# Maxima of two units in one reduction over two PSUM banks, in the last of three attention blocks

## The chip, the cores and the metric

One core of a Trainium2 chip runs the whole program. The metric is device time in microseconds, from one launch to its end. Three runs of the kernel before are shown, and one more execution was taken with a profile.

## The reference

A decoder-like stack of four layers over tokens `x` of shape (4, 256, 256). Each layer adds a gated cross-attention over a context of shape (4, 512, 256), and then a gated feed-forward, each behind a layer norm. The attentions of layers 0, 2 and 3 have 16 heads of 16 columns; that of layer 1 is a plain memory read. The feed-forwards of layers 0, 1 and 3 are mixtures of experts, that of layer 2 has weights of signs. What the change touches most is the attention of layer 3:

```python
def rms_norm(x, g, eps=EPS): ...
ctx_img, ctx_txt = context[:, :IMG_LEN], context[:, IMG_LEN:]      # IMG_LEN = 257 of 512
q = rms_norm(x @ Wq + bq, gq).reshape(b, -1, n, d)
k = rms_norm(ctx_txt @ Wk + bk, gk).reshape(b, -1, n, d)
k_img = rms_norm(ctx_img @ Wk_img + bk_img, gk_img).reshape(b, -1, n, d)
img_x = _attend(q, k_img, v_img)              # softmax over 257 keys
txt_x = _attend(q, k, v, k_mask)              # another softmax over 255 keys
out = (txt_x + img_x).reshape(b, -1, n * d)
return out @ Wo + bo
```

There are two softmaxes per query and head, one over the first 257 keys and one over the other 255, and so two maxima.

## The kernel before

The whole stack is one program. Tokens stay in SBUF; every block is written as a list of steps, and each engine runs through the same list and does its own part of each step, in that order. Nothing else orders the work but semaphores. Blocks are numbered 0 to 3, batches (of 256 tokens) `c` or `b` 0 to 3.

**Attention.** A batch has `UNITS_OF_BATCH` = 32 units of each of two kinds:

- Maxima, step `("mx", b, k)`: TensorE multiplies one tile of 128 queries of one head with all 512 keys into one PSUM bank (L886), and VectorE reduces the bank to its negated maximum. In block 3 (`two`) that is two reductions, over columns 0 to 256 (L1368) and 257 to 511 (L1369); in block 2 it is one over 512 (L1371). Block 0 has no maxima.
- Scores, step `("sc", c, u)`: the product turned round (keys on partitions, L877), of which ScalarE takes the exponential (L1059, L1061). Four units further on, `("wg", c, part)` multiplies the exponentials with the values (L910); in block 3 a `wg` has 16 or 24 small matmuls in turn. `ev` copies the sums out.

The maxima run `LAG` = 26 units ahead of the scores, since they take a detour: `ng` (VectorE splits them in two halves of precision), `nt` (TensorE turns them), `ne` (ScalarE copies), `nw` (SyncE writes them to DRAM), `nr` (GpSimd reads them back into rows beside the queries, so that the score matmul subtracts them). This is done once for each half of a batch.

Around these the list has the preparation of the next batches: `ln`, `lm` (layer norm; its root is taken by GpSimd), `xt`, `xe` (turned tokens), `kp`, `sq`, `ms`, `kk`, `tk`, `te` (keys in natural order, squares, root by GpSimd, normalization at L1289, turned), `q`, `tq`, `qe` (queries), `v`, `ve` (values), `kw`, `qw` (SyncE writes keys and queries to DRAM), `kr`, `qr` (GpSimd loads them back, the last index is the half). `("qr", 0, 1)` is followed on GpSimd's queue by a memset of the other query buffer (L628) and loads of constant rows. Behind the scores come `dt`, `dd` (sums turned, divided), `ot`, `oe`, `wo`, `wd` (projection out).

**Positions.** `order(blk)` gives each step a number and sorts: `mx` k of batch c stands at 32c + k, `sc` u at 32c + u + 26.5, `wg` at 4 part + 33.6. Preparation stands at 32c plus the offset in `PREP`, for batch 1 with `FIRST_SHIFT` added; the steps after the scores at an offset in `FINISH`. `FOLLOW` places the statistics, the transposes and the routing of the next feed-forward. Steps in `LEADS` are run early, between the tiles of the feed-forward before; `HOOKS` puts the first and last steps of an attention between tiles of a feed-forward, and `MISC` holds the small offsets.

**Banks.** A step that fills PSUM takes the next bank of its ring. `RING_A[3]` = (2, 3) serves `mx`, `dt` and `wo`, `RING_B[3]` = (5, 6, 7) the other fills. `emptied(blk, fill)` names the event that gives a bank back, and the next fill of that bank waits for it on TensorE (`wait_bank`). For a maxima unit this is its own last reduction, counted in `mx_done`.

Of the kernel before, what the change touches and what calls it, by code (L numbers as in the profile page):

```python
# [37 lines left out]
M = 512  # L38
# [53 lines left out]
def hooks(first, *lists):  # L92
# [12 lines left out]
HOOKS = [{0: [("late", "ot"), ("late", "oe")], 1: [("late", "wo")], 2: [("late", "wd"), ("late", "wr")],  # L105
         3: [("late", "wn")], 4: [("statistics", 1)], 5: [("normal", 1)],
         6: [("turn", 1), ("halves", 1)], 7: [("logits", 1)], 8: [("route", 1, 0)],
         9: [("route", 1, 1)], 10: [("route", 1, 2)], 11: [("weights", 1)], 12: [("combine", 1)],
         15: [("add", 0)], 16: [("mem", "scale"), ("extra", 0), ("extra", 1)],
         17: [("mem", "round")], 18: [("mem", "diag")], 19: [("mem", "whole")],  # L110
         20: [("mem", "spread")], 21: [("mem", "normal")], 22: [("mem", "turn")],
         23: [("mem", "context0")], 24: [("mem", "context1")], 25: [("mem", "mask")],
         26: [("mem", "kept")]},
         {-1: [("logits", 0), ("route", 0, 0), ("route", 0, 1), ("route", 0, 2)],
         0: [("weights", 0), ("combine", 0)], 1: [("statistics", 1)],
         2: [("normal", 1), ("turn", 1)], 3: [("halves", 1), ("logits", 1)], 4: [("route", 1, 0)],
         5: [("route", 1, 1)], 6: [("route", 1, 2)], 7: [("weights", 1)], 8: [("combine", 1)],
         11: [("add", 0)]},
         {0: [("late", "ot"), ("late", "oe")], 1: [("late", "wo")], 2: [("late", "wd")],
# [3 lines left out]
         3: [("statistics", 1)], 4: [("normal", 1)], 5: [("turn", 1)], 6: [("halves", 1)],  # L123
         7: [("logits", 1)], 8: [("route", 1, 0)], 9: [("route", 1, 1)], 10: [("route", 1, 2)],
         11: [("weights", 1)], 12: [("combine", 1)], 26: [("add", 0)]}]
# [180 lines left out]
def emptied(blk, fill):  # L306
# [29 lines left out]
    if name == "wo":  # L336
        return "wo_done", ("wd", b)
# [2506 lines left out]
```

How the kernel before makes its waits and increments, by code:

```python
    def wait(eng, kind, n):  # L596
        if isinstance(n, int) and n <= 0:
            return
        eng.wait_ge(sems[kind], n)
# [1 line left out]
    def link(eng, name, ins):  # L602
        chain[name] += 1
        ins.then_inc(sems[name], 1)
        eng.wait_ge(sems[name], chain[name])
# [20 lines left out]
    def zero_stack(eng, stack):  # L627
        then(eng.memset(stack[:, :].bitcast(F32), 0.0), "q_zeroed")
        zeroed[0] += 1
        eng.wait_ge(sems["q_zeroed"], zeroed[0])
# [23 lines left out]
        def w(eng, kind, n):  # L654
            if kind[:2] == "f_":
                ff_wait(eng, blk, kind, n)
            elif n > 0:
                eng.wait_ge(sems[kind], n + before_attention("pw" if kind[:2] == "pw" else kind, blk))
# [71 lines left out]
        def wait_loaded(eng, b, ph):  # L731
            eng.wait_ge(sems[f"d_r{buf(b)}{ph}"], landed(blk, b))
            if b < 2:
                wait(eng, f"d_au{buf(b)}", constants(blk, buf(b)))
                eng.wait_ge(sems["q_zeroed"], {0: 2, 2: 3 + b, 3: 4 + min(b, 1)}[blk])
                eng.wait_ge(sems["s_zeroed"], 1)
# [12 lines left out]
            def wait_weights(mat):  # L750
                if blk == 0:
                    eng.wait_ge(sems["w0_l"], {WK: 1, WQ: 2, WV: 3, WO: 4}[mat])
                    if mat in (WV, WO):
                        eng.wait_ge(sems["bias_l"], 2)
                elif blk == 2:
                    eng.wait_ge(sems["w2_l"], 2)
                    eng.wait_ge(sems["bias_l"], 2)
                    if mat == WQ:
                        eng.wait_ge(sems["q_tc"], 2)
```

## Time and profile before

| | us |
|---|---|
| median of three runs | 1186.84 |
| lowest and highest | 1183.28, 1188.63 |
| the profiled execution | 1182.87 |
| its span, first to last instruction | 1181.0 |

The mean granted TensorE clock of the profiled execution was 0.945 of full speed. Durations and starts below come from this one execution; starts count from the beginning of the span. The last attention block takes its maxima from about 742 to 912, and the feed-forward before it ends near 730.

### The profile page before, as it was taken

The numbers are of one execution on the slowest core, as the hardware profiler recorded it, in microseconds if no ns is written. First come the engines' busy times: TensorE is split into PE (matmuls) and PEld (weight loads), VectorE is DVE, ScalarE is ACT, GpSimd is POOL, SyncE is SP. The second block draws the span as 40 slices with busy tenths as digits, with TensorE's granted clock in tenths as the row PEclk, the third lists the DMA queues.
The fourth block names the chain that finished last, engine by engine and source line by source line (L and its number), as shares of the span: only waits on it lengthen the run. The fifth ranks groups of instructions, "written<-read, shape, count | busy, mean of one in ns | idle before, by whom it ended". The sixth has DMA issues, their size and how long they took to land.

```text
span 1181.0 us, 19127 instructions
## 1 busy us (share of the span) xinstructions
PE 1021.6 (87%) x6456; PEld 767.5 (65%) x6456; DVE 800.9 (68%) x1639; ACT 570.5 (48%) x1129; POOL 380.6 (32%) x423
## 2 busy tenths in 40 slices
PE   4799878999888897779999876699999989999998
PEld 3566546877766686655665565365655578887887
DVE  6477759567866367578887675677766365676676
ACT  2677753444433343316567543146555545444443
POOL 5312214355303245331211231422110043554553
PEclk8999989999988899879999998699999999999999
DMA  6957523554320277685640254927240144555544
GB/s 201 260 134 171 124 71 103 168 156 126 116 90 4 80 140 189 168 155 136 140 98 21 68 107 134 193 54 172 86 92 4 30 132 123 157 153 159 147 151 129
DMA packets 87050, 145.85 MB, mean 124 GB/s; under 512 B 10413, under 2 KB 42438, under 8 KB 84538
## 3 DMA queue, kind: packets, MB, share of 16 engines
q1 hardware_dynamic: 77562, 111.36, 31.6%
q0 software_dynamic: 9408, 33.45, 15.9%
q8 instruction: 47, 0.77, 0.3%
q14 instruction: 33, 0.27, 0.1%
HBM read 113.41 MB, written 32.41 MB: 123 GB/s over the span
## 4 chain that ended last, share of the span: by engine, by line
PE 54%; DVE 16%; DMA 9%; issue 7%; ACT 6%; POOL 5%; SPq 2%; DVEq 0%; ACTq 0%; POOLq 0%
PE psum L617 33%; PE psum L910 6%; PE psum L877 5%; PE psum L886 5%; DMA ff_raw<-in_ff 5%; ACT probs L1059 2%; DMA weights_out<-combine 2%; DVE nmx L1371 1%; POOL ff_wl L1955 1%; DVE nmx L1368 1%; DVE nmx L1369 1%; DVE ff_s L1994 1%; PE psum L836 1%; POOL keys L1122 1%; DMA keys<-keys_out 1%
## 5 line engine op out<-in xcount | busy, mean ns | idle before, releaser
L617 PE MATMUL psum<-ff_xh,ff_wh 128*128 128x512 f32 x424 | 177.7, 419 | 33.9 <-POOL ff_wl L1955 29.9
L2011 DVE TENSOR_TENSOR ff_hl<-ff_h,ff_hh 128x512 fp32r<-128x512 f32 x114 | 121.8, 1069 | 98.4 <-ACT ff_hh L1896 97.8
L1061 ACT ACTIVATE probs<-psum 128x512 f32<-128x512 f32 x256 | 144.6, 597 | 86.1 <-PE psum L877 82.3
L1955 POOL TENSOR_TENSOR ff_wl<-ff_raw,ff_wh 128x512 fp32r<-128x512 f32 x92 | 120.5, 1310 | 173.2 <-ACT ff_wh L1907 173.1
L877 PE MATMUL psum<-queries,keys 128*128 128x512 f32 x384 | 153.4, 429 | 12.2 <-ACT probs L1059 7.4
L617 PE MATMUL psum<-ff_xh,ff_wl 128*128 128x512 f32 x392 | 157.1, 401 | 0.0
L1907 ACT ACTIVATE ff_wh<-ff_raw 128x512 fp32r<-128x512 f32 x92 | 58.0, 630 | 183.1 <-DMA ff_raw<-in_ff 181.0
L617 PE MATMUL psum<-ff_wh,ff_hh 128*128 128x256 f32 x456 | 131.5, 292 | 10.3 <-DVE ff_hl L2011 10.3
L886 PE MATMUL psum<-keys,queries 128*128 128x512 f32 x256 | 119.6, 484 | 15.6 <-DVE nmx L1369 8.9
L617 PE MATMUL psum<-ff_wh,ff_hl 128*128 128x256 f32 x456 | 130.5, 290 | 0.0
L617 PEld LDWEIGHTS psum<-ff_xh,ff_wh 128*128 128x128 f32 x424 | 83.3, 196 | 58.0 <-POOL ff_wl L1955 35.9
L1960 POOL TENSOR_TENSOR ff_wl<-ff_raw,ff_wh 128x256 fp32r<-128x256 f32 x92 | 90.3, 982 | 75.1 <-ACT ff_wh L1914 73.9
L1994 DVE TENSOR_TENSOR ff_s<-ff_s,ff_w 128x512 f32<-128x512 f32 x98 | 96.7, 986 | 25.2 <-ACT ff_s L1920 18.7
L910 PE MATMUL psum<-probs,values 128*32 128x256 f32 x1664 | 111.6, 390 | 2.1 <-DVE probs L1462 1.9
L617 PE MATMUL psum<-ff_wl,ff_hh 128*128 128x256 f32 x392 | 113.4, 289 | 0.0
L617 PEld LDWEIGHTS psum<-ff_wh,ff_hh 128*128 128x128 f32 x456 | 91.1, 200 | 19.1 <-issue 12.9
L877 PEld LDWEIGHTS psum<-queries,keys 128*128 128x128 f32 x384 | 69.4, 189 | 51.2 <-ACT probs L1059 22.6
L886 PEld LDWEIGHTS psum<-keys,queries 128*128 128x128 f32 x256 | 51.2, 203 | 64.5 <-DVE nmx L1369 31.0
L1059 ACT ACTIVATE probs<-psum,aug 128x512 f32<-128x512 f32 x128 | 80.9, 692 | 24.2 <-PE psum L877 23.9
L617 PEld LDWEIGHTS psum<-ff_wh,ff_hl 128*128 128x128 f32 x456 | 90.6, 199 | 0.5
L1896 ACT ACTIVATE ff_hh<-ff_h 128x512 fp32r<-128x512 f32 x114 | 70.9, 622 | 35.5 <-DVE ff_h L2000 31.6
L1371 DVE TENSOR_REDUCE nmx<-psum 128x1 f32<-128x512 f32 x128 | 80.6, 682 | 10.7 <-PE psum L886 10.5
(263 smaller groups left out, 2154.8 us busy)
## 6 DMA issues: line engine op xcount, KB each, us to landing
ff_w<-weights_out SPq DMA_DIRECT2D x94, 256.0 KB
ff_raw<-in_ff SPq DMA_DIRECT2D x92, 256.0 KB, 3.6
keys_out<-keys_turned SPq DMA_DIRECT2D x36, 512.0 KB, 4.4
keys<-keys_out POOLq DMA_DIRECT2D x48, 384.0 KB, 7.5
ff_raw<-in_ff SPq DMA_DIRECT2D x106, 128.0 KB, 2.1
queries_out<-queries_turned SPq DMA_DIRECT2D x36, 256.0 KB, 3.2
queries<-queries_out POOLq DMA_DIRECT2D x32, 256.0 KB, 4.3
w_raw<-in_w SPq DMA_DIRECT2D x12, 256.0 KB, 3.7
```

The lines of the kernel that those rows point to most:

```text
L617: last = eng.matmul(dst, lhs[i](k), rhs[j](k), start=start and n == 0, stop=stop and n == groups * len(pairs) - 1, skip_group_check=True)
L877: then(eng.matmul(dst, kst[buf(c)][:, pair, kt * P:(kt + 1) * P], qst[buf(c)][:, :, pair, :], start=True, stop=True, skip_group_check=True ...
L886: then(eng.matmul(bank(st), qst[buf(b)][:, m, pair, qt * P:(qt + 1) * P], kst[buf(b)][:, pair, :], start=True, stop=True), "mx_full")
L910: last = eng.matmul(psum[32 * j:32 * j + 32, SUM_BANK, col:col + S], values[:, c % 2, slot, h * VW:h * VW + 32], probs[:, n % 3, i, j, :], ...
L1059: ins = eng.activation(dst, src, ACT.Exp, scale=SCALE, bias=aug0[:, KT * c + kt:KT * c + kt + 1])
L1061: ins = eng.activation(dst, src, ACT.Exp, scale=SCALE)
L1371: ins = eng.tensor_reduce(at_(0), bank(st), AX.X, ALU.max, negate=True)
L1896: then(eng.activation(ff_hh[:, slot, :], ff_h[:, slot, :], ACT.Copy), "f_hh")
L1955: then(eng.tensor_tensor(ff_wl[:, slot, 0:2 * D], raw(n, slot)[:, 0:2 * D], ff_wh[:, slot, 0:2 * D].bitcast(F32), ALU.subtract), "f_w1r")
L1960: then(eng.tensor_tensor(ff_wl[:, slot, 2 * D:3 * D], raw(n, slot)[:, BD:BD + D], ff_wh[:, slot, BD:BD + D].bitcast(F32), ALU.subtract), " ...
L1994: then(eng.tensor_tensor(ff_s[:, slot, :], ff_s[:, slot, :], ff_w[:, slot, :], ALU.mult), "f_sw")
L2011: then(eng.tensor_tensor(ff_hl[:, slot, :], ff_h[:, slot, :], ff_hh[:, slot, :].bitcast(F32), ALU.subtract), "f_hr")
```

## The change

In block 3 the two units of a pair (k even and k odd) get neighbouring places, at the odd one's position, and lie in banks 2 and 3. VectorE does nothing at the even unit. At the odd one it takes the maximum over columns 0 to 256 of both banks in one reduction with an output of 128 x 2, and then the same for columns 257 to 511. Both banks count as emptied when both reductions of the pair are over. Where the ring is shifted by an odd number of `wo` fills, the even unit lies in bank 3; TensorE then takes the tile of queries that belongs to the bank (`qt = plan.bank[st] - min(RING_A[blk])`). The number of maxima matmuls is the same; 256 reductions become 128.

Besides, positions change in every block: hooks in all four feed-forwards, offsets of preparation, of loads from DRAM and of values in blocks 0, 2 and 3, the shift of batch 1 in block 3 from -6.6 to +3.2, and the place of the routing. In the order that results for block 3, the loads of batch 0 (`kr`, `qr`) and the maxima 0 and 1 stand ahead of `xt`, `kp` and the rest of batch 1; the even and odd maxima are followed by two scores each time; `ct` stands behind the last `wg`. No step is added or dropped.

```diff
-         {0: [("late", "ot"), ("late", "oe")], 1: [("late", "wo")], 2: [("late", "wd")],
+         {0: [("late", "ot")], 1: [("late", "oe")], 2: [("late", "wo"), ("late", "wd")],
...
-         3: [("statistics", 1)], 4: [("normal", 1)], 5: [("turn", 1)], 6: [("halves", 1)],
-         7: [("logits", 1)], 8: [("route", 1, 0)], 9: [("route", 1, 1)], 10: [("route", 1, 2)],
-         11: [("weights", 1)], 12: [("combine", 1)], 26: [("add", 0)]}]
+         3: [("statistics", 1), ("normal", 1)], 4: [("turn", 1)], 5: [("halves", 1)],
+         6: [("logits", 1)], 7: [("route", 1, 0)], 8: [("route", 1, 1)], 9: [("route", 1, 2)],
+         10: [("weights", 1)], 12: [("combine", 1)], 26: [("add", 0)]}]
...
-        ("qr", 0, -8.8), ("kr", 1, -0.5), ("qr", 1, -8.3), ("v", 0, 5.2), ("ve", 0, 5.8), ("v", 1, 8.2),
+        ("qr", 0, -4.8), ("kr", 1, 5.9), ("qr", 1, -1.9), ("v", 0, 7.6), ("ve", 0, 8.2), ("v", 1, 10.6),
...
-        ("kr", 0, -12), ("qr", 0, -13.4), ("kr", 1, -0.5), ("qr", 1, -1.5), ("v", 0, 19.5), ("ve", 0, 20.1),
-        ("v", 1, 22.5), ("ve", 1, 32.3)],
+        ("kk", 2, -22), ("tq", None, -19.2), ("qe", None, -18.6), ("qw", None, -17.2), ("kr", 0, -14.4),
+        ("qr", 0, -13.4), ("kr", 1, 7.5), ("qr", 1, -1.5), ("v", 0, 19.5), ("ve", 0, 20.1), ("v", 1, 23.7),
+        ("ve", 1, 25.7)],
 }
-FIRST_SHIFT = {0: -16.4, 2: -14, 3: -6.6}
+FIRST_SHIFT = {0: -16.4, 2: -14, 3: 3.2}
...
-FOLLOW = {0: (17.6, 4.6, 18.8), 2: (26.2, 9.2, 0), 3: (25.6, 9.2, 23.2)}
+FOLLOW = {0: (17.6, 4.6, 20), 2: (30.2, 9.2, 0), 3: (25.6, 9.2, 25.6)}
...
-                at(r + k, "mx", c, k)
+
+                at(r + (k // 2 * 2 + 1 - (1 - k % 2) * .005 if blk == 3 else k), "mx", c, k)
...
         return "wo_done", ("wd", b)
+    if blk == 3:
+
+        return "mx_done", ("mx", b, rest[0] | 1)
     return "mx_done", fill
...
             def maxima(st):
                 _, b, k = st
                 pair, m, qt = k // 4, k // 2 % 2, k % 2
+                if two:
+
+                    qt = plan.bank[st] - min(RING_A[blk])
...
-                if b and k % HALF_UNITS == 0:
+                if two and qt == 0:
+                    return
+                if b and k // 2 * 2 % HALF_UNITS == 0:
                     w(eng, "neg_done", HALVES * (b - 1) + ph + 1)
                 filled(eng, st)
 
-                def at_(part):
-                    i = (part * JJ + jj) * QT + qt
-                    return nmx[:, ph, m, i:i + 1]
-
                 if two:
-                    eng.tensor_reduce(at_(0), bank(st)[:, 0:IMG], AX.X, ALU.max, negate=True)
-                    ins = eng.tensor_reduce(at_(1), bank(st)[:, IMG:M], AX.X, ALU.max, negate=True)
+                    banks = psum[:, min(RING_A[blk]):min(RING_A[blk]) + QT, :]
+                    i = jj * QT
+                    then(eng.tensor_reduce(nmx[:, ph, m, i:i + QT], banks[:, :, 0:IMG], AX.X, ALU.max, negate=True),
+                         "mx_done")
+                    i += JJ * QT
+                    ins = eng.tensor_reduce(nmx[:, ph, m, i:i + QT], banks[:, :, IMG:M], AX.X, ALU.max, negate=True)
                 else:
-                    ins = eng.tensor_reduce(at_(0), bank(st), AX.X, ALU.max, negate=True)
+                    i = jj * QT + qt
+                    ins = eng.tensor_reduce(nmx[:, ph, m, i:i + 1], bank(st), AX.X, ALU.max, negate=True)
                 then(ins, "mx_done")
```

## Rows read from the trace of the kernel before

**Rows 1.** The page: busy time of each engine, its share, its instructions.

```profile
PE 1021.6 (87%) x6456; PEld 767.5 (65%) x6456; DVE 800.9 (68%) x1639; ACT 570.5 (48%) x1129; POOL 380.6 (32%) x423
```

**Rows 2.** Windows: us, busy (x) PE PEld DVE ACT POOL, PEclk, DMA share, GB/s.

```profile
742.00:760.00 18.00, 10.51 (x35) 6.22 (x33) 11.23 (x32) 1.96 (x7) 6.75 (x10) 0.62 0.98 208
781.00:912.00 131.00, 122.79 (x977) 78.29 (x977) 94.17 (x277) 75.79 (x159) 21.52 (x40) 1.00 0.33 80
```

**Rows 3.** Waits in 781:912: us in total, times, longest.

```profile
PEld psum L886 <- DVE nmx L1369: 17.6, 36, 1.3
```

**Rows 4.** Timeline, 813 to 821: two groups of four units (start, length, engine).

```profile
813.59 0.50 PE L886 MATMUL psum<-keys,queries 128*128 128x512 f32 x1
...
817.26 0.50 PE L886 MATMUL psum<-keys,queries 128*128 128x512 f32 x1
...
817.60 0.40 PE L877 MATMUL psum<-queries,keys 128*128 128x512 f32 x1
...
817.80 0.42 DVE L1368 TENSOR_REDUCE nmx<-psum 128x1 f32<-128x257 f32 x1 [0.90 <-PE psum L886]
817.84 0.39 PE L886 MATMUL psum<-keys,queries 128*128 128x512 f32 x1
...
818.14 0.41 DVE L1369 TENSOR_REDUCE nmx<-psum 128x1 f32<-128x255 f32 x1
...
818.61 0.50 PE L886 MATMUL psum<-keys,queries 128*128 128x512 f32 x1
...
819.94 1.50 PE L910 MATMUL psum<-probs,values 128*32 128x256 f32 x24
...
821.37 0.50 PE L886 MATMUL psum<-keys,queries 128*128 128x512 f32 x1
```

**Rows 5.** Lines by form on VectorE: block 2's reduction and the last block's first.

```profile
L1371 DVE TENSOR_REDUCE nmx<-psum 128x1 f32<-128x512 f32 x128 | 80.6, 682 | 10.7 <-PE psum L886 10.5
...
L1368 DVE TENSOR_REDUCE nmx<-psum 128x1 f32<-128x257 f32 x128 | 54.7, 436 | 37.6 <-PE psum L886 37.2
```

**Rows 6.** Timeline, 872 to 880: the units around the turned outputs.

```profile
872.91 0.50 PE L886 MATMUL psum<-keys,queries 128*128 128x512 f32 x1
...
879.63 0.50 PE L886 MATMUL psum<-keys,queries 128*128 128x512 f32 x1
```

**Rows 7.** Timeline of SyncE's queue, 716 to 750.

```profile
721.89 1.41 SPq L1516 DMA_DIRECT2D queries_out<-queries_turned  x3
```

**Rows 8.** Transfers from issue to landing, 710 to 745 (KB each, median us).

```profile
queries<-queries_out POOLq DMA_DIRECT2D x4, 256.0 KB, 3.9
...
keys<-keys_out POOLq DMA_DIRECT2D x2, 384.0 KB, 7.0
```

**Rows 9.** Timeline of the opening of the last attention block, 731 to 749.

```profile
731.41 0.69 POOL L1113 TENSOR_TENSOR rstd<-ve,half_neg 128x2 f32<-128x2 f32 x1 [12.99 <-DVE ve L1254]
732.06 1.15 POOL L1122 DMA_DIRECT2D queries<-queries_out  x2
732.14 0.73 DVE L1262 TENSOR_SCALAR xn<-x,mv,rstd 128x256 f32<-128x256 f32 x2 [0.81 <-POOL rstd L1113]
...
740.33 3.56 POOL L628 MEMSET queries<- 128x4096 f32 x1
...
741.61 0.73 PE L886 MATMUL psum<-keys,queries 128*128 128x512 f32 x2 [0.99 <-DMA keys<-keys_out]
...
742.15 1.77 DVE L1368 TENSOR_REDUCE nmx<-psum 128x1 f32<-128x257 f32 x1
...
748.49 0.88 DVE L1289 SCALAR_TENSOR_TENSOR kn<-psum,rms,rows 128x256 f32<-128x256 f32 x2 [4.57 <-POOL rms L1116]
```

**Rows 10.** Timeline of TensorE, 753 to 762: two maxima matmuls, low clock.

```profile
757.43 1.45 PE L886 MATMUL psum<-keys,queries 128*128 128x512 f32 x2 [1.13 <-DVE nmx L1369]
```

**Rows 11.** Timeline of ScalarE: the block's first exponentials.

```profile
776.84 1.28 ACT L1061 ACTIVATE probs<-psum 128x512 f32<-128x512 f32 x2 [6.12 <-PE psum L877]
```

**Rows 12.** Timeline of TensorE before the last feed-forward.

```profile
942.72 0.60 PE L1721 MATMUL psum<-ident_r,rt_c 128*17 128x128 f32 x4 [0.48 <-DVE rt_c L1706]
```

More of the change, by code:

```diff
@@ L101 @@
         3: ("ot", "oe", "wo", "wd")}
[L105 to L113, printed above, removed]
+HOOKS = [{0: [("late", "ot"), ("late", "oe")], 1: [("late", "wo")], 3: [("late", "wd"), ("late", "wr")],
+         4: [("late", "wn")], 5: [("statistics", 1), ("normal", 1)],
+         6: [("turn", 1), ("halves", 1)], 8: [("logits", 1), ("route", 1, 0), ("route", 1, 1)],
+         10: [("route", 1, 2)], 11: [("weights", 1)], 12: [("combine", 1)], 15: [("add", 0)],
+         16: [("mem", "scale"), ("extra", 0), ("extra", 1)], 17: [("mem", "round")],
+         18: [("mem", "diag"), ("mem", "whole")], 19: [("mem", "spread")], 20: [("mem", "normal")],
+         21: [("mem", "turn")], 22: [("mem", "context0")], 23: [("mem", "context1")],
+         24: [("mem", "mask")], 25: [("mem", "kept")]},
          {-1: [("logits", 0), ("route", 0, 0), ("route", 0, 1), ("route", 0, 2)],
-         0: [("weights", 0), ("combine", 0)], 1: [("statistics", 1)],
-         2: [("normal", 1), ("turn", 1)], 3: [("halves", 1), ("logits", 1)], 4: [("route", 1, 0)],
-         5: [("route", 1, 1)], 6: [("route", 1, 2)], 7: [("weights", 1)], 8: [("combine", 1)],
+         0: [("weights", 0), ("combine", 0), ("statistics", 1)], 1: [("normal", 1)],
+         2: [("turn", 1), ("halves", 1)], 3: [("logits", 1)], 4: [("route", 1, 0)],
+         5: [("route", 1, 1)], 6: [("route", 1, 2)], 7: [("weights", 1)], 9: [("combine", 1)],
          11: [("add", 0)]},
-         {0: [("late", "ot"), ("late", "oe")], 1: [("late", "wo")], 2: [("late", "wd")],
+         {0: [("late", "ot")], 1: [("late", "oe")], 2: [("late", "wo"), ("late", "wd")],
          3: [("late", "wn")], 4: [("statistics", 1)], 5: [("normal", 1), ("extra", 0)],
@@ L225, in check_order @@
     assert asked == taken, blk
-MISC = {"au": -20, "ng": 0.3, "nt": 1.8, "ne": 2.3, "nw": 2.4, "nr": 2.5, "cl": 1.4, "ev": 0.3, "fx": 3.5, "fw": 3, "fv": 32, "fe": 1.2, "lg": 4, "ro1": 1.5, "ro2": 3.5, "ct": 6, "ce": 6.8}
+MISC = {"au": -20, "ng": 0.9, "nt": 2.1, "ne": 2.3, "nw": 2.4, "nr": 2.5, "cl": 1.4, "ev": 0.3, "fx": 3.5, "fw": 3, "fv": 32, "fe": 1.2, "lg": 4, "ro1": 1.5, "ro2": 3.5, "ct": 6, "ce": 6.8}
 def order(blk):
```

17 rows, old and new, of tables (FINISH, LEADS, PREP) are left out of this document.

## The prediction

> **What bounds the kernel now.** I read the page first: TensorE is busy 87% of the span and VectorE 68% [rows 1]. That is an average over seven blocks, and the main edit touches only the stretch in which the last attention block takes its maxima, so I read that stretch by windows [rows 2]. The reader should see two different regimes. From 742 to 760 TensorE is busy 10.5 of 18 us at a granted clock of 0.62, the DMA engines are busy 98% of the time, and VectorE is not full either: a latency regime. From 781 to 912 TensorE is busy 94% of the time at a clock of 1.00 and VectorE 72%: TensorE's queue is nearly full there, and what it loses it loses in short waits. The view of waits names the main one: 36 times, 17.6 us in all, a weight load for a maxima matmul waited for VectorE's second reduction [rows 3]. The timeline then shows how that wait works [rows 4].
>
> **A group of four units before.** A maxima matmul starts at 817.26, VectorE starts to read at 817.80, its two reads start 0.34 apart, the second ends at 818.55, and at 818.61 TensorE refills the same bank [rows 4]. While VectorE reads one bank TensorE fills the other, so with VectorE limiting a unit costs 2 x 0.34 = 0.67 us. The group from 813.59 to 817.26, with the shorter weighing, takes 3.67 us, the one from 817.26 to 821.37, with the longer, 4.11 us. In the weighing (819.94 to 821.37, 1.43 us) VectorE runs dry and TensorE works.
>
> **Part 1, the reads themselves.** 128 units x 2 reads become 64 x 2, of twice the width. A read of 257 has a mean of 436 ns and one of 512 of 682 ns [rows 5], about 0.96 ns a column, so from the 0.34 us spacing of two 257-column reads a 514-column read should keep VectorE 0.34 + 257 x 0.00096 = 0.59 us, call it 0.60. A pair of units then costs 1.20 us of VectorE for 1.34, which is 0.14 x 64 = 9 us of VectorE time over the block, but VectorE is the limit in only part of it. Bounds: 0.68 a read (two banks cost the same as two reads; saving nothing) and 0.55.
>
> The Trainium skill, page "VectorE: DVE Perf Modes", section on the TRN2 errata, gives a read from PSUM as 120 cycles plus one per element at 0.96 GHz: an estimate from it is 0.39 us for 257 and 0.66 us for 514, so 0.25 us saved per pair and 16 us over 64 pairs. The recorded lengths agree with it (0.41 to 0.42 for 257), but the spacing of 0.34 shows that reads overlap, and so the saving by that page is too high.
>
> **Part 2, the ring of two banks.** The price of the wide read: it needs both banks full, and neither may be refilled until both reads are over (a unit's release is now the odd unit's). From the first matmul of a pair: the second starts 0.34 later [rows 4], is done about 0.40 after that (a matmul that follows another: 0.40, same rows), VectorE starts 0.04 after that, reads for 0.60 + 0.68, and TensorE goes on 0.06 later: 0.78 + 1.28 + 0.06 = 2.12 us from pair to pair, whatever TensorE has in between. Two units cost 1.34 before. In between the new order gives TensorE two score matmuls and, in every other pair, a weighing. With four matmuls at 0.23 to 0.34 (817.26, 817.60, 817.84 [rows 4]) and a weighing of 1.43 a pair takes about 2.5 (TensorE's own), with two scores alone 2.12 (1.2 of it idle). The shorter weighing (1.0) makes it 2.12 too. So a group goes from 4.11 to 2.5 + 2.12 = 4.6, and from 3.67 to 4.24: about +0.5 each. I went through the new order of 781 to 912, 24 groups: some 12 have nothing but scores and weighings (+6 us). Some 8 have a projection, keys or values in the bare pair, which hides the wait entirely and also the 0.3 to 0.4 us waited there now (-3). In two batches turned outputs share the ring with the maxima. There a pair, a turned output, its division on VectorE and the next pair go one after the other: 872.91 to 879.63 holds four units in 6.7 us [rows 6], and by the same steps I get 10.1 (two stretches, one half covered by a projection: +5.5). Sum +8.5 us; bounds +3 (fillers cover more) and +16 (all 24 groups +0.5, both output stretches in full, reads at 0.68).
>
> **Part 3, the opening.** The new order (values of PREP and FIRST_SHIFT) has the key and query loads of batch 0 ahead of the statistics on GpSimd's queue, and the maxima of batch 0 ahead of the preparation of batch 1 on TensorE's. Now: the queries are out by 721.89 + 1.41 plus landing [rows 7], GpSimd has been idle for 13 us, and still the load goes out at 732.06, since GpSimd waits for the root of the layer norm; keys land 7.0 us after issue, queries 3.9 [rows 8]; the first maxima matmul waits for that until 741.61 and VectorE first reads at 742.15 [rows 9]. After: the keys can go at about 720 and the queries at about 727, so both are in by 731; TensorE has no other work then, and VectorE is free after its normalization, at 732.14 + 0.73 = 732.9. That is 9.3 us earlier. The memset of 3.56 us and its loads, which stand now between a request and its root and leave VectorE idle for 4.57 us before 748.49, move ahead to about 733, where no root is asked for: -4.6. Against that: 13 pairs before the first score instead of 26 single units. About 7 have preparation behind them, 6 do not. At the low clock two maxima matmuls take 1.45 us [rows 10] and a pair takes 1.45 + 1.28 + 0.06 = 2.8 instead of the 1.65 of now: 6 x 1.15 = +6.9, or 6 x 0.78 = +4.7 at the full clock; I take +6. The preparation that VectorE did before 742 (two subtractions of 512 columns, by the nearest row 0.68 each [rows 5], a normalization like the 0.88 at 748.49, a small request) now stands in its queue between maxima: +2.4. The narrower reads: 13 x 0.14 = -1.8. Sum -9.3 - 4.6 + 6 + 2.4 - 1.8 = -7.3, I take -7.5. The first exponential, now at 776.84 [rows 11], needs the first half of the maxima back from DRAM; even with no idle time on VectorE it could not come before some 765, so the gain is at most 12; below, 3 if the clock stays low throughout.
>
> **Part 4, the rest.** The turn of the routing weights goes behind the last weighing: the 0.60 us and the 0.48 us of wait in front of it [rows 12] leave the path to the first loads of the last feed-forward, -1 us (0 to -1.1). The loads of the second halves of the keys are asked for about 8 to 10 units later than now; eight units are some 9 to 10 us against a landing of 7.0: hidden, and 1 to 3 us per batch if not. The moves of hooks in the four feed-forwards and of a few reads in blocks 0 and 2 shift an equal set of instructions by one tile or a few units; nothing is added or removed, and the nearby work covers them: 0, bounds -3 and +3.
>
> **The sum**: -7.5 + 8.5 - 1 + 0 = 0 on the profiled execution of 1182.87 us (span 1181.0). The median of the runs shown is 1186.84, 4.0 above it, and it is on this that I put the forecast: 1186 us.
>
> **The rivals.** Faster: the ring costs little (+2, the fillers cover nearly all bare pairs and VectorE's relief helps the work queued behind it) and the opening gives its upper end (-11): 1186.8 + 2 - 11 - 1 = 1177. For it speaks that preparation and weighings are spread through the order and that VectorE stands at 72%; against it the count of bare pairs. Slower, by the clock: TensorE now idles 1 us in every second pair, and if the clock, 1.00 from 781 to 912, falls to its lower level there, two maxima matmuls that take 0.34 + 0.40 = 0.74 at the full clock take 1.45 [rows 10]. From 742 to 760 the clock was 0.62 with TensorE busy 58%. Twenty us of it at half speed cost 10: 1196. It decides from about 12 us on. Against it: the busy share would fall only to some 85%. The Trainium skill, page "TensorE: Matmul & The Clock Gate", section "A second HAM failure mode: psum-queue depth-cycling", says that cycling through PSUM banks with small idles between groups of matmuls makes the clock swing; this is that pattern. Slower, by the loads: the second halves of the keys come 2 us late in three batches, +6, so 1193. That the wide read saves nothing (0.68) is inside the range of part 2.
>
> **How the numbers follow.** Forecast 0.44 (1181 to 1192), faster rival 0.31, clock 0.15, late loads 0.10. What a measurement of this kernel can tell from no change is about 0.5%, 6 us. Faster 0.31, same 0.44, slower 0.25. The range goes from 1174, a little beyond the faster case, to 1199, beyond the clock.
>
> **What would show it.** Part 1: wide reads spaced 0.59 to 0.61 apart. Part 2: pairs of maxima matmuls 2.1 us apart with only scores between, 781 to 912 lengthened from 131 to about 139. Part 3: the first maxima reduction near 733, the first exponential of the block near 768 instead of 777, no 4.57 us wait for the root. The prediction is wrong if the clock falls below 1.00 in the middle of the block, if the wide reads take under 0.5 or over 0.7, or if the opening keeps waiting for the keys.

## The result and the profile after

The change made the kernel faster: 1172.36 us median (1169.49 to 1180.05, 4 runs) against 1185.07 us (1183.28 to 1188.63, 4 runs) for the kernel before beside it, a ratio of 0.990 [0.985, 0.995]. A second measurement of the same kernel, below, gave 0.992 [0.989, 0.995]. The forecast was 1186 us, no difference to be measured; its range began at 1174, and the time lies just under it. The profiled execution after took 1180.05 us (span 1178.2), the longest of its four, so lengths of stages are compared here and the totals are left to the medians.

The lines of after answer to those of before so: maxima matmul L886 to L892, first and second reduction L1368 and L1369 to L1374 and L1377, scores L877 to L880, weighing L910 to L916, and L617, the matmul of the feed-forwards and projections, to L620. The page of after (busy time, share, instructions), for [rows 1]:

```profile
PE 1017.6 (86%) x6456; PEld 768.6 (65%) x6456; DVE 796.2 (68%) x1511; ACT 571.3 (48%) x1129; POOL 383.1 (33%) x423
```

VectorE has 128 instructions fewer, and TensorE has as many as before. The averages say nothing of where the time went, so I cut both executions at the same events. The end of a feed-forward is here the start of VectorE's last product in it (`ff_h`), and the last feed-forward is counted from its first such product to its last. Stage lengths in us, worked out from these events in the two timelines:

```
stage                                                     before   after   after - before
start to the memset ahead of feed-forward 1                368.5   365.4    -3.1
feed-forward 1, from that memset to its end                131.6   118.4   -13.2
block 2: end of feed-forward 1 to last maxima              138.6   137.8    -0.8
block 2: last maxima to end of feed-forward 2               83.7    83.6    -0.1
last block, opening: to the first maxima reduction          19.8    14.7    -5.1
last block, lead: to the first exponential                  34.7    32.6    -2.1
last block, middle: to the last maxima reduction           135.8   153.5   +17.7
last block, tail: to the last feed-forward                  44.1    43.8    -0.3
last feed-forward                                          216.2   220.2    +4.0
```

The last block as a whole is 10 us longer. The gain is in feed-forward 1, which the prediction had at nothing. The first and last stages vary between executions of kernels that are the same there (the first took 365.4, 367.1 and 372.7 us in experiments 5, 6 and 3 below, the last 215.6 in the second profile of the changed kernel), so they carry no argument. The eight us behind the last stage hold the last matmuls, the addition and the store.

**The opening and the lead.** Timeline of after, 713 to 722, against [rows 9]:

```profile
713.10 1.07 POOL L1128 DMA_DIRECT2D queries<-queries_out  x2 [8.88 <-DMA queries_out<-queries_turned]
...
714.32 0.71 POOL L1119 TENSOR_TENSOR rstd<-ve,half_neg 128x2 f32<-128x2 f32 x1 [0.16 <-DVE ve L1260]
...
716.06 3.55 POOL L631 MEMSET queries<- 128x4096 f32 x1
...
720.00 0.68 DVE L1374 TENSOR_REDUCE nmx<-psum 128x2 f32<-128x514 f32 x1
```

The load now stands ahead of the root and waits for nothing but its data (8.88 us idle, ended by the store of the queries). The memset starts 10.8 us behind the end of the feed-forward (705.3) where it stood 18.0 behind it (722.4) before. The first read comes at 720.00, and the first exponential at 752.62, so the two stages are 7.2 us shorter. The store of the queries takes longer to land than it did. Transfers (KB each, median us from issue to landing), 716 to 750 of before and then 699 to 725 of after:

```profile
queries_out<-queries_turned SPq DMA_DIRECT2D x3, 256.0 KB, 2.5
```

```profile
queries_out<-queries_turned SPq DMA_DIRECT2D x3, 256.0 KB, 6.3
```

In after the load of the keys, asked for at 703.11, is under way at the same time. No run separates the two transfers, so that this is the reason is not shown.

**The middle.** Windows of after (columns as in [rows 2]):

```profile
752.00:780.00 28.00, 23.86 (x187) 16.36 (x185) 19.74 (x39) 16.69 (x41) 6.07 (x12) 1.00 0.28 63
780.00:810.00 30.00, 23.50 (x170) 14.86 (x163) 14.19 (x29) 13.75 (x27) 4.96 (x9) 0.89 0.61 139
810.00:840.00 30.00, 26.67 (x214) 17.78 (x213) 21.55 (x47) 16.53 (x40) 4.72 (x9) 1.00 0.39 109
840.00:870.00 30.00, 24.90 (x197) 16.08 (x199) 16.82 (x32) 14.30 (x27) 6.25 (x12) 0.99 0.48 92
870.00:906.00 36.00, 32.37 (x243) 19.57 (x235) 22.81 (x47) 19.61 (x37) 2.05 (x3) 0.96 0.01 3
```

TensorE is busy 131.3 of 154 us where before had 127.3 of 136 (window 777 to 913): its idle time went from 9 to 23 us. The granted clock, 1.00 before, falls to 0.89 between 780 and 810 and to 0.96 behind 870. Timeline of one pair with little behind it (two scores and a short transpose, L851), and below the one matmul that waited for a load:

```profile
835.23 0.62 PE L892 MATMUL psum<-keys,queries 128*128 128x512 f32 x2
...
835.89 0.69 DVE L1374 TENSOR_REDUCE nmx<-psum 128x2 f32<-128x514 f32 x1 [0.67 <-PE psum L892]
...
836.50 0.68 DVE L1377 TENSOR_REDUCE nmx<-psum 128x2 f32<-128x510 f32 x1
...
837.32 0.70 PE L892 MATMUL psum<-keys,queries 128*128 128x512 f32 x2 [0.22 <-DVE nmx L1377]
```

```profile
785.72 1.22 PE L892 MATMUL psum<-keys,queries 128*128 128x512 f32 x2 [3.67 <-DMA keys<-keys_out]
```

From pair to pair it is 2.09 us; 852.71 and 854.73 in the same trace are 2.02 apart. VectorE, which paced the units before, now waits for TensorE (0.67 us here) as TensorE waits for VectorE. The reads by form (busy, mean ns, idle before), for [rows 5]:

```profile
L1374 DVE TENSOR_REDUCE nmx<-psum 128x2 f32<-128x514 f32 x64 | 44.3, 692 | 52.4 <-PE psum L892 51.5
L1377 DVE TENSOR_REDUCE nmx<-psum 128x2 f32<-128x510 f32 x64 | 43.4, 678 | 0.0
```

In all 64 pairs the second read starts 0.60 to 0.61 us after the first.

The fall of the clock behind 870 has no load ahead of it. It stands where turned outputs and maxima share the two banks; the row is the second of two such waits, the windows are the low stretches at the load and here:

```profile
868.07 0.63 PE L839 MATMUL psum<-ident_r,o_t 128*128 128x128 f32 x4 [1.47 <-DVE nmx L1377]
```

```profile
784.10:790.70 6.60, 4.99 (x23) 2.90 (x24) 1.29 (x2) 1.36 (x3) 0.42 (x1) 0.50 0.57 191
869.40:872.60 3.20, 3.20 (x26) 1.79 (x18) 0.25 (x2) 0.38 (x2) 0.00 (x0) 0.50 0.03 0
```

**Feed-forward 1.** Timeline of before, 389 to 405, which the prediction did not look at:

```profile
389.36 0.69 DVE L1994 TENSOR_TENSOR ff_s<-ff_s,ff_w 128x512 f32<-128x512 f32 x1 [2.87 <-DMA ff_w<-weights_out]
390.09 0.69 DVE L2000 TENSOR_TENSOR ff_h<-ff_s,psum 128x512 f32<-128x512 f32 x1
390.69 1.38 DVE L1622 TENSOR_SCALAR ff_xn<-x,mv,rstd 128x256 f32<-128x256 f32 x4
...
391.16 2.30 PE L1631 MATMUL psum<-ident_r,ff_xn 128*128 128x128 f32 x8 [3.80 <-DVE ff_xn L1622]
...
396.30 0.69 DVE L1994 TENSOR_TENSOR ff_s<-ff_s,ff_w 128x512 f32<-128x512 f32 x1 [2.04 <-ACT ff_s L1920]
...
398.48 0.69 DVE L2000 TENSOR_TENSOR ff_h<-ff_s,psum 128x512 f32<-128x512 f32 x1 [1.49 <-PE psum L617]
...
399.08 1.28 DVE L1643 TENSOR_TENSOR ff_xl_second<-psum,ff_xh 128x512 fp32r<-128x512 f32 x2
...
400.42 0.27 PE L617 MATMUL psum<-gate_hi,ff_xh 128*128 128x8 f32 x1 [2.04 <-DVE ff_xl_second L1643]
...
403.97 0.35 PE L617 MATMUL psum<-gate_lo,ff_xh 128*128 128x8 f32 x1
404.18 0.35 PE L617 MATMUL psum<-gate_hi,ff_xl_second 128*128 128x8 f32 x1
404.40 0.77 PE L617 MATMUL psum<-ff_xh,ff_wh 128*128 128x512 f32 x1
```

The normalization of the second token half stands in the same tile as its turn on TensorE. On VectorE's queue it is behind two steps of the feed-forward, the first of which waited 2.87 us for weights from DRAM. So TensorE stood still for 3.80 us. One tile on the halves stand in the same tile as the logits, behind the next two products on VectorE, which had waited 2.04 us for ScalarE and 1.49 for TensorE; the logits wait 2.04 us for the halves. Of the 24 gate matmuls behind that wait the first 12 start 0.11 us apart and the last 12, from 401.83 on, 0.21. The same events in after, timeline of TensorE:

```profile
383.97 1.03 PE L1640 MATMUL psum<-ident_r,ff_xn 128*128 128x128 f32 x8
...
389.05 0.17 PE L620 MATMUL psum<-gate_hi,ff_xh 128*128 128x8 f32 x1
...
391.20 0.25 PE L620 MATMUL psum<-gate_hi,ff_xl_second 128*128 128x8 f32 x1
391.31 0.25 PE L620 MATMUL psum<-gate_hi,ff_xh 128*128 128x8 f32 x1
```

Neither has a wait, and the gate matmuls are 0.11 apart. The windows of the 20 us from the gate matmuls on, and the stretches at the lower level of 1.2 GHz, first of before, then of after:

```profile
400.00:420.00 20.00, 19.58 (x101) 17.61 (x102) 8.59 (x18) 7.70 (x13) 5.92 (x6) 0.83 0.29 83
401.80:408.40 6.60, 6.60 (x27) 6.02 (x27) 0.36 (x1) 0.60 (x1) 0.00 (x0) 0.50 0.15 46
391.60:394.80 3.20, 3.20 (x11) 2.63 (x12) 1.74 (x3) 1.15 (x2) 1.27 (x1) 0.50 0.61 164
```

```profile
389.05:409.05 20.00, 20.00 (x117) 17.90 (x116) 13.35 (x31) 10.61 (x19) 8.72 (x8) 0.91 0.47 131
391.60:394.80 3.20, 3.20 (x10) 2.62 (x11) 2.00 (x3) 1.29 (x3) 1.35 (x2) 0.50 0.42 106
```

TensorE is busy nearly all the time in both. The granted clock is 0.83 against 0.91: before is low twice, once behind each wait, and after is low once, from the end of its gate matmuls on and with no wait ahead. Over the whole feed-forward, before and then after:

```profile
368.50:500.10 131.60, 108.67 (x563) 92.15 (x564) 76.89 (x154) 47.98 (x91) 54.49 (x51) 0.90 0.52 125
```

```profile
365.50:483.80 118.30, 104.30 (x562) 88.89 (x563) 77.24 (x154) 48.16 (x91) 54.59 (x51) 0.93 0.55 139
```

TensorE's idle time went from 22.9 to 14.0 us, of which the two waits are 5.8; another 2.9 are waits for weights that GpSimd splits (14.6 us before, 11.7 after). Its busy time went from 108.7 to 104.3 with the clock. These two executions are one draw: experiment 3, with the old hooks, took 128.8 us here, and the nine profiles of kernels with the new hooks other than after took 117.0 to 121.3.

### The profile page after: what moved, and what is told of

It reads as the page before. It is cut to its first block, busy times and chain, and to the rows that moved or that the text cites. A ratio compares the mean times of both kernels' runs of the same rounds, so it can differ in the third digit from the quotient of the medians.

```text
span 1178.2 us, 19005 instructions
## 1 busy us (share of the span) xinstructions
PE 1017.6 (86%) x6456; PEld 768.6 (65%) x6456; DVE 796.2 (68%) x1511; ACT 571.3 (48%) x1129; POOL 383.1 (33%) x423
## 4 chain that ended last, share of the span: by engine, by line
PE 57%; DVE 15%; DMA 11%; issue 6%; ACT 5%; POOL 4%; SPq 2%; DVEq 0%; ACTq 0%; POOLq 0%
PE psum L620 34%; PE psum L916 7%; PE psum L880 6%; PE psum L892 6%; DMA ff_raw<-in_ff 5%; DMA keys<-keys_out 2%; DVE nmx L1374 2%; ACT probs L1065 1%; DVE nmx L1377 1%; DMA weights_out<-combine 1%; POOL ff_wl L1964 1%; PE psum L839 1%; DMA queries_out<-queries_turned 1%; DVE ff_s L2003 1%; DVE nmx L1380 1%
## 5 line engine op out<-in xcount | busy, mean ns | idle before, releaser
L620 PE MATMUL psum<-ff_xh,ff_wh 128*128 128x512 f32 x424 | 176.8, 417 | 25.9 <-POOL ff_wl L1964 21.6
L2020 DVE TENSOR_TENSOR ff_hl<-ff_h,ff_hh 128x512 fp32r<-128x512 f32 x114 | 119.0, 1044 | 99.7 <-ACT ff_hh L1905 99.0
L880 PE MATMUL psum<-queries,keys 128*128 128x512 f32 x384 | 158.2, 445 | 16.3 <-DMA keys<-keys_out 5.6
L620 PE MATMUL psum<-ff_xh,ff_wl 128*128 128x512 f32 x392 | 156.7, 400 | 0.0
L620 PE MATMUL psum<-ff_wh,ff_hh 128*128 128x256 f32 x456 | 130.5, 290 | 10.3 <-DVE ff_hl L2020 10.2
L892 PE MATMUL psum<-keys,queries 128*128 128x512 f32 x256 | 105.0, 460 | 34.4 <-DVE nmx L1377 17.7
L620 PE MATMUL psum<-ff_wh,ff_hl 128*128 128x256 f32 x456 | 129.4, 288 | 0.0
L880 PEld LDWEIGHTS psum<-queries,keys 128*128 128x128 f32 x384 | 70.1, 192 | 70.7 <-ACT probs L1067 26.5
L916 PE MATMUL psum<-probs,values 128*32 128x256 f32 x1664 | 114.0, 398 | 1.7 <-DVE probs L1471 1.7
L620 PEld LDWEIGHTS psum<-ff_xh,ff_wh 128*128 128x128 f32 x424 | 83.0, 196 | 49.6 <-POOL ff_wl L1964 26.2
L620 PE MATMUL psum<-ff_wl,ff_hh 128*128 128x256 f32 x392 | 112.6, 287 | 0.0
L2003 DVE TENSOR_TENSOR ff_s<-ff_s,ff_w 128x512 f32<-128x512 f32 x98 | 96.3, 983 | 14.7 <-DMA ff_w<-weights_out 7.7
L620 PEld LDWEIGHTS psum<-ff_wh,ff_hh 128*128 128x128 f32 x456 | 89.7, 197 | 18.9 <-issue 13.8
L892 PEld LDWEIGHTS psum<-keys,queries 128*128 128x128 f32 x256 | 48.8, 204 | 64.9 <-DVE nmx L1377 22.4
L620 PEld LDWEIGHTS psum<-ff_wh,ff_hl 128*128 128x128 f32 x456 | 89.5, 196 | 0.5
```

The costliest lines, as they stand in the source:

```text
L620: last = eng.matmul(dst, lhs[i](k), rhs[j](k), start=start and n == 0, stop=stop and n == groups * len(pairs) - 1, skip_group_check=True)
L880: then(eng.matmul(dst, kst[buf(c)][:, pair, kt * P:(kt + 1) * P], qst[buf(c)][:, :, pair, :], start=True, stop=True, skip_group_check=True ...
L892: then(eng.matmul(bank(st), qst[buf(b)][:, m, pair, qt * P:(qt + 1) * P], kst[buf(b)][:, pair, :], start=True, stop=True), "mx_full")
L916: last = eng.matmul(psum[32 * j:32 * j + 32, SUM_BANK, col:col + S], values[:, c % 2, slot, h * VW:h * VW + 32], probs[:, n % 3, i, j, :], ...
L2003: then(eng.tensor_tensor(ff_s[:, slot, :], ff_s[:, slot, :], ff_w[:, slot, :], ALU.mult), "f_sw")
L2020: then(eng.tensor_tensor(ff_hl[:, slot, :], ff_h[:, slot, :], ff_hh[:, slot, :].bitcast(F32), ALU.subtract), "f_hr")
```

## The experiments

Two theories after the result. A: the gain comes from the hooks of feed-forward 1, and the last block loses. B: it comes from the last block. Medians are beside runs of the kernel before on the same chip (1186.16, 1183.31 and 1185.23 us in the three sets of four), so the ratios are what is to be compared.

**1. Only the hooks of feed-forward 1 moved**, all else as before:

```
-         0: [("weights", 0), ("combine", 0)], 1: [("statistics", 1)],
-         2: [("normal", 1), ("turn", 1)], 3: [("halves", 1), ("logits", 1)], ... 8: [("combine", 1)],
+         0: [("weights", 0), ("combine", 0), ("statistics", 1)], 1: [("normal", 1)],
+         2: [("turn", 1), ("halves", 1)], 3: [("logits", 1)], ... 9: [("combine", 1)],
```

> The kernel before with only the hooks of the second feed-forward (feed-forward 1) placed as in the changed kernel: statistics, normalization, transposes, halves and logits of the second half of the tokens are each one tile apart from the step that needs them. Theory A (the gain lies in the hooks of feed-forward 1, where TensorE waited 3.8 us for normalized tokens and 2.0 us for their low halves and then ran at the low clock): about 1173 to 1177 us, 8 to 12 us under the kernel before, all of it between the start of feed-forward 1 and its end. Theory B (the gain comes from the last attention block, by earlier loads and wide reads): no difference, 1183 to 1187.

1174.37 us, ratio 0.991 [0.988, 0.994]; feed-forward 1 took 119.5 us. Within the uncertainty this is as much as the whole change gains.

**2. Every change outside the last block**, that block with its old places (but for the split and turn of the maxima, `ng` and `nt`, whose offsets hold for blocks 2 and 3) and single reads:

> The kernel before with every edit outside the last attention block: hooks of feed-forwards 0, 1 and 2, preparation offsets of blocks 0 and 2, the places of routing there, and the small shift of the maxima's split and turn. Theory A (the gain lies outside the last block, 16 to 17 us of it in the profile): 1167 to 1172. Theory B (the gain comes from the last block): 1182 to 1187.

1169.56 us, 0.986 [0.982, 0.991]. Feed-forward 1 took 119.3 and the middle of the last block 135.1. The other hooks and places add at most a few us; the interval overlaps that of experiment 1.

**3. Only the last block's changes:**

> The kernel before with the wide reductions and all places of the last block (and of the last feed-forward), and nothing else. Theory A: the last block as a whole is slower, by 5 to 10 us where its clock falls and by 0 to 3 us where not: 1185 to 1195. Theory B: 1172 to 1178.

1201.29 us, 1.012 [1.008, 1.016], with a middle of 157.2 us: slower, and by more than I expected. In this version the turn of the maxima stays ahead of the next pair, and TensorE also waits for their halves (3.5 us in four waits, in the view of waits of 774 to 932). It waits 1.8 us for keys, and the clock is 0.89 from 774 to 838. B falls.

**4. The changed kernel with single reads of one bank**, each unit at its own place, and all other changes kept:

> The changed kernel with all its new places, but with the maxima one unit at a time (two reductions per unit, each bank given back alone, units at their old numbers). Theory A (the ring of two banks costs more than the wide read saves): 3 to 8 us faster than the changed kernel, 1165 to 1170, with clock 1.00 in the middle of the last block. Theory B (the wide read is what gains): 5 us or more slower than the changed kernel, above 1177.

1170.33 us, 0.989 [0.985, 0.992]. The profile has a middle of 144.1 us where the wide reads had 153.5 (152.0 in the second profile), but the medians are 2 us apart and the intervals overlap. The wide reads gain nothing in their own places; how much they lose there the times do not settle, the profiles say 8 to 9 us. The clock was not 1.00, as I had expected of single reads. One matmul waits 2.6 us for keys here too, and the windows from 751 to 809 are low:

```profile
751.00:780.00 29.00, 26.83 (x190) 17.66 (x188) 22.51 (x66) 17.58 (x40) 6.40 (x12) 0.94 0.26 63
780.00:809.00 29.00, 26.11 (x192) 17.43 (x193) 17.16 (x54) 15.40 (x34) 5.79 (x11) 0.88 0.57 138
```

So of the 17.7 us that the middle gained, some 8 (144.1 less 135.8) come with the new places, the late load and the clock, without any wide read.

**5 and 6. The two halves of experiment 1.** In 5 only the normalization goes one tile ahead of its turn (and the statistics one tile ahead of it). In 6 only the halves go one tile ahead of the logits:

```
5: 0: [("weights", 0), ("combine", 0), ("statistics", 1)], 1: [("normal", 1)], 2: [("turn", 1)],
   3: [("halves", 1), ("logits", 1)]
6: 0: [("weights", 0), ("combine", 0)], 1: [("statistics", 1)], 2: [("normal", 1), ("turn", 1), ("halves", 1)],
   3: [("logits", 1)]
```

> The kernel before, with one edit in feed-forward 1: the normalization of the second token half one tile ahead of its turn, halves and logits still in one tile. Theory (two separate stalls and their clock): the 3.80 us wait for the normalized tokens goes, the 2.04 us wait for the token halves and the low clock behind it stay, so feed-forward 1 is 4 to 7 us shorter than the 131.6 of before and the time 1179 to 1182 beside 1186. Rival (one cause, the clock): the first stall is what brings the clock down for all that follows, so this edit alone gives the whole 12 us, 1174. Second rival: the remaining wait takes over all that the first gave, 1185 or more.

> The kernel before, with one edit in feed-forward 1: the halves of the turned tokens one tile ahead of the logits, normalization and turn still in one tile. Theory: the 2.04 us wait goes, and the small gate matmuls and the tile after them run at the full clock (some 3 to 4 us), the 3.80 us wait stays: 4 to 7 us, so 1179 to 1182. Rival (the first stall sets the clock): the gate matmuls stay at the lower clock and only 2 us come back, 1184. The two edits together gave 1174.

5: 1181.27 us, 0.9985 [0.996, 1.001]. 6: 1178.29 us, 0.996 [0.994, 0.998]. Together they are worth 0.9% and apart 0.15 and 0.4%. For 5 the trace shows why. Timeline and the window behind it:

```profile
384.10 1.04 PE L1631 MATMUL psum<-ident_r,ff_xn 128*128 128x128 f32 x8
...
389.43 1.34 DVE L2011 TENSOR_TENSOR ff_hl<-ff_h,ff_hh 128x512 fp32r<-128x512 f32 x1 [2.05 <-ACT ff_hh L1896]
...
392.55 1.28 DVE L1643 TENSOR_TENSOR ff_xl_second<-psum,ff_xh 128x512 fp32r<-128x512 f32 x2
...
393.88 0.38 PE L617 MATMUL psum<-gate_hi,ff_xh 128*128 128x8 f32 x1 [4.54 <-DVE ff_xl_second L1643]
```

```profile
394.00:414.00 20.00, 20.00 (x101) 18.03 (x102) 8.02 (x17) 7.86 (x13) 5.07 (x5) 0.80 0.24 77
```

The turn is 7 us earlier (3 of them from the stages ahead) and waits for nothing, but the halves still stand on VectorE's queue behind the products of the feed-forward, one of which waited 2.05 us for ScalarE. The wait moved one step on and grew from 2.04 to 4.54 us, and the clock behind it is low (0.80). In 6 the first wait stays and the second goes:

```profile
390.30 2.12 PE L1631 MATMUL psum<-ident_r,ff_xn 128*128 128x128 f32 x8 [3.69 <-DVE ff_xn L1622]
...
397.65 0.17 PE L617 MATMUL psum<-gate_hi,ff_xh 128*128 128x8 f32 x1
```

```profile
399.00:419.00 20.00, 19.85 (x118) 17.24 (x118) 12.66 (x30) 10.13 (x18) 8.38 (x8) 1.00 0.42 132
```

The clock is back at 1.00 by the gate matmuls, although 3.69 us of standing still came before. Feed-forward 1 took 125.1 us in the profile of 5 and 120.9 in that of 6. Both profiled executions are the fastest of their kernels, so these two lengths are on the low side. Even so 120.9 lies among the 117.0 to 121.3 of the kernels with both edits: that 6 lacks half of the gain is seen in its median alone, and its interval touches that of experiment 1. The rival that the first wait alone sets the clock for all that follows is wrong; the second rival, that the remaining wait takes over what the first gave, holds for 5.

**7. Experiment 2 with wide reads and paired units**, the last block's places otherwise as before:

> All hooks and places of the changed kernel outside the last block, the last block's places as before, but the wide reads with their pairs of units. Against the same kernel with narrow reads (1169.6). Theory (the ring of two banks costs more than VectorE gains): the stretch from the first exponential of the last block to its last maxima goes from 135 to 143 to 150 us, the time is 1177 to 1184. Rival (the wide read is free, only the new places in that block cost): 135 to 138 us and 1167 to 1172. Second rival (it saves VectorE time that counts): under 1166.

1186.75 us, 1.004 [1.001, 1.006], against 0.986: the wide read costs 1.7%, some 20 us, in the places of before. The lead took 39.3 us where experiment 2 had 33.9, and the middle 151.1 where it had 135.1. TensorE's work in the middle is nearly the same, its idle time is not. Windows of the middle, 7 and then 2:

```profile
762.00:913.00 151.00, 130.84 (x993) 85.80 (x993) 94.95 (x190) 80.61 (x168) 21.45 (x40) 0.97 0.29 71
```

```profile
758.00:894.00 136.00, 128.40 (x994) 81.10 (x993) 99.58 (x294) 80.33 (x168) 21.51 (x40) 1.00 0.37 85
```

Idle: 20.2 us against 7.6. TensorE's clock is 0.82 from 762 to 790 in 7 (0.62 in the lead before), which by this share is about 5 of the 16 us.

**8. Experiment 2 with the two matmuls of a pair side by side, but single reads**, to tell the places from the read:

```
-                at(r + k, "mx", c, k)
+                at(r + (k // 2 * 2 + 1 - (1 - k % 2) * .005 if blk == 3 else k), "mx", c, k)
```

> Against the kernel with the changed places outside the last block (0.986 of before) one edit: in the last block the two maxima matmuls of a pair stand side by side in the order, as the wide read needs them, but VectorE still reads each bank by itself and gives it back at once. Theory A (the cost of the wide read is that neither bank comes back before both reads are over): little is lost, middle of the block 135 to 139 us, time 1167 to 1172. Rival B (the places side by side cost, not the read): middle 145 us or more, as with the wide read (151), time 1178 to 1187.

1170.20 us, 0.990 [0.986, 0.993], middle 138.4 us. The pairing alone costs 3.3 us of the middle, part of it in score matmuls that now stand side by side and wait for the exponential (weight loads wait 8.1 us in 19 waits in this middle, 0.5 in one in that of experiment 2). The other 12.7 us of experiment 7 come with the wide read itself, which gives no bank back before both reads are over, about 5 of them as the low clock at the start. Theory A of this run holds.

**9. Experiment 2 with the new opening only:**

```
+FIRST_OUT = {("qw", None): -36, ("kr", 0): -35.5, ("qr", 0): -35}
-FIRST_SHIFT = {0: -16.4, 2: -14, 3: -6.6}
+FIRST_SHIFT = {0: -16.4, 2: -14, 3: 0}
...
+            if blk == 3 and c == 0 and (name, arg) in FIRST_OUT:
+                early_ = FIRST_OUT[name, arg]
```

> The kernel with the changed places outside the last block and narrow reads there (1169.6), and of the last block's changes only the opening: first keys and queries of batch 0 loaded ahead of the statistics of batch 1, whose preparation goes 6.6 positions later. Theory (the opening is worth what it was worth in the changed kernel, and the middle isn't touched): last feed-forward tile to first maxima 14 to 16 us instead of 20, lead 32 to 34, middle 135 to 138, time 1161 to 1166. Rival (an early start is given back, because batch 1's preparation now stands between the maxima): opening shorter, lead longer by as much, 1168 to 1171.

1159.74 us (1155.73 to 1165.84), 0.979 [0.976, 0.982]: faster than both kernels; on the changed one the ratios make it 13 to 16 us. Opening 16.3, lead 32.2, middle 135.5. In the profiles the opening and the lead give 5.4 us over experiment 2, the medians 9, with intervals that just fail to touch.

**10. The same with the early loads only**, batch 1's preparation left where it was:

> Against the kernel with the changed places outside the last block: only the first keys and queries of batch 0 are loaded ahead of the statistics of batch 1; the preparation of batch 1 stays where it was. Theory (the load behind the root is what held the maxima): most of the 5 to 7 us of the version that also moves the preparation, so 1161 to 1165. Rival (the preparation of batch 1 on TensorE and VectorE then stands in front of the first maxima and takes the place of the load): opening 19 to 20 us, time 1167 to 1170.

1163.30 us, 0.981 [0.978, 0.985]. The profile shows the rival: opening 20.6 us, lead 33.8, no gain over the 20.0 and 33.9 of experiment 2, since the preparation still stands ahead of the maxima. The median lies between those of 2 and 9 and its interval touches both. That the move of the preparation is needed is therefore shown in the profiles and not by the times.

**11. The changed kernel with the load of the second half of the keys 8 positions earlier**, `("kr", 1, -0.5)` for `("kr", 1, 7.5)`, **and 12. the changed kernel once more:**

> The changed kernel with one number back: the loads of the second halves of the keys are asked for 8 positions earlier, as before. Theory (the one wait of 3.7 to 4.0 us for keys in the middle of the block is a true cost): 3 to 4 us faster than the changed kernel, about 1168. Rival (the wait is covered, since the next waits take over or the load falls among others): no difference, 1171 to 1173.

> The changed kernel once more, for a second profile and a closer ratio beside the versions above. Theory (VectorE's idle time behind the wide reads and the clock that falls with TensorE's waits): middle of the last block again 150 us or more, granted clock under 1.00 in part of it, ratio 0.985 to 0.993. Rival (the fall of the clock was particular to that one execution, which was the longest of its kernel): clock 1.00 all through, middle about 145 us.

11: 1170.68 us, 0.989 [0.985, 0.993], middle 146.7 us. 12: 1175.65 us, 0.992 [0.989, 0.995], middle 152.0 us. The ratios overlap, so the time is not settled; the profiles are clear. In 12 TensorE waits 3.5 us once for the keys, as in the first profile of this kernel, and then comes the lower clock. In 11 that wait is gone, and the window at the same place has the clock at 1.00. The windows, of 12 and then of 11:

```profile
787.00:818.00 31.00, 25.45 (x189) 16.89 (x190) 14.74 (x31) 14.24 (x32) 5.43 (x10) 0.89 0.50 111
```

```profile
778.00:807.00 29.00, 25.82 (x211) 17.80 (x211) 17.51 (x37) 15.30 (x33) 8.04 (x15) 1.00 0.60 119
```

Between these two profiles the middle differs by 5.3 us: some 3.5 waited for the late load, the rest with the clock.

## Why the prediction was wrong

**The step that failed** is in part 4: "The moves of hooks in the four feed-forwards [...] shift an equal set of instructions by one tile or a few units; nothing is added or removed, and the nearby work covers them: 0, bounds -3 and +3." It measured -13.2 us in feed-forward 1. From its memset to the turn -4.1, to the first gate matmul -4.2, over the gate matmuls -1.2, to the end -3.7; of the last part 2.9 are shorter waits for split weights, which vary between executions. That the work covers them was assumed for all four feed-forwards without a row of any. The waits of 3.80 and 2.04 us stood in the trace of before at exactly the two hooks that the change separates, and a step in the same tile as its consumer on another engine is where such a wait is to be looked for. Experiment 1 shows that these hooks alone give the gain, and 5 that moving only the first step does not; whether the second alone falls short (6) is likely by the medians and not settled.

**Part 1** was right: 0.60 us from read to read, measured 0.60 to 0.61 in 64 of 64. The page "VectorE: DVE Perf Modes" of the Trainium skill (section on the TRN2 errata) would have had 0.25 us saved per pair of units; by the spacings it is 1.34 less 1.22, or 0.12 us, so the trace does not agree with its fixed cost per read once reads follow each other.

**Part 2** was right in mechanism, and its size fits. Pair to pair was forecast at 2.12 us and measured 2.00 to 2.13 with scores alone or the shorter weighing in between. The stretch of [rows 6] was forecast to grow from 6.7 to 10.1; in after it goes from the pair at 861.80 to the one at 872.51, 10.7 us, of which 1.5 are the low clock from 869 (in experiment 11, at 1.00, the same stretch took 9.2). The ring is worth 8 to 9.4 us in the middle by the profiles (152.0 and 153.5 against the 144.1 of experiment 4, all three with the late load), where +8.5 was forecast. The +10.9 of experiment 11 (146.7 against 135.8) also holds the other new places. In the old places the same read costs 16.0 in the middle, at the upper bound of 16, and 5.4 more in the lead (experiment 7 against 2), which no term had.

**Part 3** was right in its sum, -7.5 forecast and -7.2 measured (-6.5 in the second profile), but by luck: two of its terms were off and cancelled. The first read was to come 9.3 us earlier, and counted from the end of the feed-forward it came 5.1 earlier (14.7 us behind it instead of 19.8). The prediction had the load of the queries go at about 727, 4.6 us behind the end of the feed-forward; it went at 713.10, 7.8 behind it, since the store ahead of it took 6.3 us to land instead of 2.5. The rest of part 3 (-4.6 + 6 + 2.4 - 1.8) was to make the lead 2.0 longer, and it is 2.1 shorter (1.5 in the second profile). The wait of 4.57 us at the root is gone and the memset stands where it was forecast, so the costs of pairs and preparation in the lead were sized too high; which of them the runs do not say.

**The rest of part 4**: the turn of the routing weights waits for nothing now, as said. The tail is 0.3 us shorter, too little to tell from none.

**The rivals.** The late loads (0.10) happened, as one wait of 3.5 to 3.7 us instead of three of 2, and with single reads too (2.6 us, experiment 4). The clock (0.15) fell as well, which the prediction had named as a sign of being wrong: for 6.8 us around that load in both profiles of the changed kernel, and in the first also for 3.4 us where turned outputs share the ring, behind two waits of 1.47 us for VectorE and no load. The same happened in experiment 3. In experiment 11, with the same ring and the same two waits, the whole middle was at 1.00 with 19 of 146 us idle. So a low stretch stands behind the ring's waits in two of the five profiles with wide reads, for 3.4 us where the rival had 20; the longer one stands at the load. The rule on depth-cycling of "TensorE: Matmul & The Clock Gate" in the Trainium skill names such small idles between groups of matmuls, and these traces neither bear it out nor rule it out. In experiment 7 the ring was there too and the clock was 0.82 from 762 to 790, behind a lead at 0.62; what held it down there stays open.

Both rivals belong to one addition, not to separate cases. The middle cost 16.2 to 17.7 us: about 8 to 9 for the ring and about 8 for the new places with the late load and its clock, where the sum had 8.5 in all. With -13 in feed-forward 1 and -7 in the opening and lead that leaves a gain of 3 us by either profile; the spans of these profiles are 3 and 7 us below that of before, and the medians say 10 to 13, with intervals of some 3 to 5 us to either side. The profiled execution of before was faster than its median and the first of after the slowest of its kernel, so the difference of two executions is too small here. The faster rival's 1177 was near the time for a wrong reason: the ring did not cost little.

## What to carry to other kernels

In a diff that moves many steps, look up in the trace of before each pair that it separates, a step and its consumer on another engine, before any of them is costed at nothing; the wait stands there with its length. A wait behind a busy queue moves to the next consumer when only the first is cleared (2.04 us became 4.54 in experiment 5), so look at both. A wide read over two banks is paid for by the ring: count what the filling engine can do until both banks are back, and where it has only two short matmuls, as here, two single reads that free each bank at once are better.

## What the hardware showed beyond that

The same 128x8 matmuls stood 0.11 us apart at a granted clock of 1.00 and 0.21 at 0.50, the two levels of 2.4 and 1.2 GHz, within one group of 24 in before. The clock was low behind or within waits of very different length: 1.8 us (experiment 3), 2.04 (before), 2.6 (experiment 4), 3.5 to 3.8 and 4.54. It was also low from 391.5 to 394.9 in after with no wait ahead, while experiment 11, whose feed-forward 1 is the same, was at 1.00 there. In experiment 6 a wait of 3.69 us was over at 390.30, and by 397.65 the small matmuls were at the short spacing again, with work in between. So no single wait decides it in these traces, and the same kernel shows a low stretch in one execution and not in the next.

Two reads of 257 columns on VectorE start 0.34 us apart, and one of 514 columns over two banks holds the next off for 0.60 to 0.61: a wider read costs its columns, and little else is saved by merging (about 0.07 us a read).
